# The slot list of an expert mixture built by TensorE products instead of 128 scattered stores, and the first expert operands loaded inside the front stage

## The reference

```python
dw = conv(q_lin, dw_w) + dw_b                     # 3 taps, by channel
off = tanh(pw_w @ gelu(dw) + pw_b) * 6
positions = clip(base + anchor + off, 0, q - 1)   # 16 heads x 12 samples
scores = qh . sample(kh, positions) / sqrt(16) - rel_scale * |rel|
out = softmax(scores) . sample(vh, positions)
...
idx = top_k(x @ Wr.T + br + biases_N, 2)          # 8 experts
h = x @ Wl1[e] + bl1[e];  a, b = halves of h      # 256 -> 2 x 512
y = (silu(a) * b) @ Wl2[e] + bl2[e]               # 512 -> 256
ffn = sum over the 2 chosen of weight * y
```

## Time and profile before

| what | value |
|---|---|
| median of 3 runs (lowest to highest) | 1495.42 us (1495.07 to 1499.51) |
| span of the profiled execution | 1494.3 us |
| what lies around its span | 1.1 us, taken as median less span; the profile gives no separate time of that execution |
| pass two of the front, steps 3 to 12 | from 165.4 to 309.9 us |
| end of the front block, first work of the mix block | 359.6 and 362.8 us |
| busy over the span | PE 91%, DVE 86%, ACT 55%, POOL 54% |
| DVE busy from 500 to 1200 us | 691.5 of 700 us |

### The profile page before, as it was taken

One profiled execution on the slowest core, in us unless ns is written; L12 is line 12 of the kernel. 1 busy time (PEld: TensorE's weight loads), 2 busy tenths in 40 slices (PEclk: granted clock), 3 DMA queues, 4 the chain that ended last, 5 costly groups with the idle time before them and its releaser, 6 DMA issues.

```text
span 1494.3 us, 35841 instructions
## 1 busy us (share of the span) xinstructions
PE 1361.6 (91%) x13687; PEld 1085.4 (73%) x13688; DVE 1280.2 (86%) x1504; ACT 823.8 (55%) x1889; POOL 804.3 (54%) x566
## 2 busy tenths in 40 slices
PE   5998899984799999999999998999999978797988
PEld 4864565653688888888888886887888856675766
DVE  7837655556699999999999999999999999999961
ACT  2547687864445555555555554554555436574655
POOL 1001477773587766767666877768686651311111
PEclk9999999985999999999999999999999988898999
DMA  7933366564957676768677666767777679999897
GB/s 231 352 130 101 115 203 208 166 222 158 287 122 224 170 232 161 222 161 235 183 204 214 168 179 160 214 159 201 196 190 221 133 178 232 250 218 246 217 246 148
DMA packets 203481, 293.52 MB, mean 196 GB/s; under 512 B 24833, under 2 KB 160261, under 8 KB 203123
## 3 DMA queue, kind: packets, MB, share of 16 engines
q0 software_dynamic: 65792, 146.59, 38.5%
q1 hardware_dynamic: 134915, 144.84, 33.6%
q10 hardware_dynamic: 2672, 0.83, 0.2%
HBM read 182.83 MB, written 117.74 MB: 201 GB/s over the span
## 4 chain that ended last, share of the span: by engine, by line
DVE 48%; DMA 8%; PE 8%; issue 6%; SPq 5%; POOL 0%; ACT 0%; POOLq 0%; DVEq 0%
DVE gslope L1647 11%; DVE parts L1643 11%; DVE parts L1603 8%; DMA band<-band_rows 7%; DVE expert_mem L1569 5%; PE pB L1480 3%; DVE parts L1615 3%; SPq L1121 2%; DVE parts L1619 2%; DVE parts L1622 1%; PE pA L1465 1%; PE pY L1490 1%; DVE gslope L1700 1%; SPq L1115 1%; DVE wgt L1708 1%
## 5 line engine op out<-in xcount | busy, mean ns | idle before, releaser
L1175 POOL DMA_INDIRECT moe_rows<-expert_mem,token_of x142 | 324.9, 2288 | 76.2 <-issue 47.9
L1446 PE MATMUL pA<-xsT,expert_mem 128*128 128x256 f32 x1136 | 264.5, 387 | 22.6 <-DMA expert_mem<-in_w_l 15.5
L1156 POOL DMA_INDIRECT expert_mem<-xn_rows,token_of x142 | 222.3, 1566 | 96.8 <-issue 74.2
L1452 PE MATMUL pY<-expert_mem 128*128 x1136 | 265.7, 387 | 0.0
L1446 PEld LDWEIGHTS pA<-xsT,expert_mem 128*128 128x128 f32 x1136 | 220.3, 195 | 55.9 <-issue 20.0
L1446 PE MATMUL pB<-xsT,expert_mem 128*128 128x256 f32 x1136 | 256.8, 379 | 0.0
L1452 PEld LDWEIGHTS pY<-expert_mem 128*128 128x128 f32 x1136 | 211.1, 191 | 42.3 <-issue 16.2
L1446 PEld LDWEIGHTS pB<-xsT,expert_mem 128*128 128x128 f32 x1136 | 215.8, 190 | 29.3
L1643 DVE SCALAR_TENSOR_TENSOR parts<-pos_pair,prob 128x768 f32<-128x768 f32 x256 | 228.0, 953 | 1.1
L1647 DVE TENSOR_REDUCE gslope<-parts 128x256 f32<-128x3072 f32 x64 | 214.7, 3354 | 2.2
L1297 ACT ACTIVATE expert_mem<-pA,b1sel 128x256 f32<-128x256 f32 x284 | 111.3, 474 | 135.3 <-issue 93.2
(11 more groups left out here) (197 smaller groups left out, 2036.3 us busy)
## 6 DMA issues: line engine op xcount, KB each, us to landing
expert_mem<-in_w_l POOLq DMA_DIRECT2D x71, 1024.0 KB, 7.0
band<-band_rows SPq DMA_DIRECT2D x256, 96.0 KB, 5.5
S_rows<-stage SPq DMA_DIRECT2D x64, 376.0 KB
band_rows<-wgt SPq DMA_DIRECT2D x12, 1536.0 KB, 7.1
pos_pair<-pos_rows SPq DMA_DIRECT2D x28, 384.0 KB, 7.7
xn_rows<-stage SPq DMA_DIRECT2D x16, 512.0 KB, 5.4
v_rows<-stage SPq DMA_DIRECT2D x16, 512.0 KB, 4.2
moe_rows<-zeros POOLq DMA_DIRECT2D x4, 2048.0 KB
```

The source lines that it names most:

```text
L1156: nc.gpsimd.indirect_dma_start(out=xs[:, u, s], out_offset=None, in_=dram["xn"], in_offset=bass.IndirectOffsetOnAxis(ap=keep["inv"][:, 2 * ...
L1175: nc.gpsimd.indirect_dma_start(out=dram["moe"], out_offset=bass.IndirectOffsetOnAxis(ap=keep["inv"][:, 2 * n + s:2 * n + s + 1], axis=0), ...
L1446: mm = nc.tensor.matmul(dst[:, c], w1[:, 1 - u, k, o * HID + c * P:o * HID + (c + 1) * P], xsT[:, k], start=(k == 0), stop=(k == KC - 1))
L1452: mm = nc.tensor.matmul(pY[:, s], hid[:, h, c, s * P:(s + 1) * P], w2[:, c, ds(e * D, D)], start=False, stop=(s == 1 and c == HC - 1))
```

## The change

One: the list is no longer written by GpSimd. In the steps 3 to 13 VectorE builds one-hot matrices of type bf16, four (choice, tile) columns at a time (a part; there are 32 parts, three in a step and two in step 13), and TensorE sums their products in the PSUM tile `pCount`: the row is the slot's low seven bits, the column its high part, one half holds the token's lane plus one and the other its tile number. In step 14 VectorE reads the sums (`tokens_of_slots`). Two: `expert_mem` is now allocated over both blocks, and shares memory with `kT` and `stage`. Inside the front GpSimd loads the first two pairs' first weights, as soon as step 7 has been scored, and gathers their rows; SyncE loads two of the four parts of `w2` in steps 8 and 9. Three: in the mix block SyncE issues the third part of `w2`, then `reload_slope(1)`, then the fourth; ScalarE starts with `evacuate_x(0)` and `take_expert(0, 0)` and does `prepare(0)` after them.

```diff
-            def scatter(some):
-                for c in some:
-                    nc.gpsimd.indirect_dma_start(
-                        out=dram["list"], out_offset=bass.IndirectOffsetOnAxis(ap=list_row[:, c:c + 1], axis=0),
-                        in_=token_i[:, c:c + 1], in_offset=None).then_inc(scattered, 16)
...
-            for q in range(4):
-                scatter(range(q * LISTED // 4, min((q + 1) * LISTED // 4, LISTED - 8)))
+            for q in range(2):
                 clear_moe(q)
-            scatter(range(LISTED - 8, LISTED))
+            pool.wait_ge(experts_known, 1)
+            pool.wait_ge(s_done, EARLY_FROM * GROUP)
+            for n in range(2):
+                e = pool.value_load(keep["tile_exp"][0:1, n:n + 1], min_val=0, max_val=EXPERTS - 1)
+                pool.dma_start(keep["w1"][:, 1 - n], io["w_l1"][ds(e, 1), :, :].rearrange("o (k p) n -> p (o k) n", p=P)).then_inc(
+                    keep["w1_loaded"][n], 16)
+            for q in range(2, 4):
+                clear_moe(q)
...
-            pool.wait_ge(scattered, 16 * LISTED)
-            pool.dma_start(spare_i[:], dram["list"].rearrange("(p n) o -> p (n o)", p=P)).then_inc(list_loaded, 16)
             pool.wait_ge(gates_stored, 16 * 4)
...
+            pool.wait_ge(tokens_known, 1)
+            for n in range(2):
+                for s in range(2):
+                    nc.gpsimd.indirect_dma_start(
+                        out=keep["xs"][:, n, s], out_offset=None, in_=dram["xn"],
...
+            def place_part(b):
+                if b < 0 or b >= LIST_PARTS:
+                    return
+                pe.wait_ge(hot_ready, b + 1)
+                for i in range(LIST_PART):
+                    mm = nc.tensor.matmul(pList, low_hot[b % 2][:, i], high_hot[b % 2][:, i].rearrange("p f n -> p (f n)"),
+                                          start=(b == 0 and i == 0), stop=(b == LIST_PARTS - 1 and i == LIST_PART - 1))
+                mm.then_inc(hot_used, 1)
...
+            def hot_part(b):
...
+                low, high, cols = low_hot[b % 2], high_hot[b % 2], slice(b * LIST_PART, (b + 1) * LIST_PART)
+                tile = b * LIST_PART % TILES
+                if b >= 2:
+                    dve.wait_ge(hot_used, b - 1)
+                V.tensor_tensor(low, place[:, None, 0:LOW].broadcast_to([P, LIST_PART, LOW]),
+                                slot_low[:, cols].unsqueeze(2).broadcast_to([P, LIST_PART, LOW]), ALU.is_equal)
+                chain(V.tensor_tensor(high[:, :, 1], place[:, None, :].broadcast_to([P, LIST_PART, HIGH]),
+                                      slot_high[:, cols].unsqueeze(2).broadcast_to([P, LIST_PART, HIGH]), ALU.is_equal))
+                chain(V.tensor_scalar(high[:, :, 0], high[:, :, 1], lane[:, 0:1], None, ALU.mult))
+                V.tensor_tensor(high[:, :, 1], high[:, :, 1], place[:, tile:tile + LIST_PART].unsqueeze(2).broadcast_to([P, LIST_PART, HIGH]),
+                                ALU.mult).then_inc(hot_ready, 1)
+
+            def tokens_of_slots():
+
+                dve.wait_ge(hot_used, LIST_PARTS)
...
+                hot_part((n - LIST_FROM) * PARTS_EACH)
                 if n + 2 < STEPS:
                     slopes_of_k(n + 2)
+                for i in range(1, PARTS_EACH):
+                    hot_part((n - LIST_FROM) * PARTS_EACH + i)
+                if n == STEPS - 2:
+                    tokens_of_slots()
...
-            sp.wait_ge(w1_loaded[0], 16)
-            for k in range(HC):
-                sp.dma_start(w2[:, k].rearrange("p (e n) -> p e n", e=EXPERTS),
-                             io["w_l2"].rearrange("e (k p) n -> k p e n", p=P)[k]).then_inc(w2_loaded, 16)
+            for k in range(EARLY_W2, HC):
+                keep["load_w2"](sp, k)
+                if k == EARLY_W2:
+                    reload_slope(1)
...
-            prepare(0)
             evacuate_x(0)
             take_expert(0, 0)
+            prepare(0)
```

More of the change, by code:

```diff
@@ L65 @@
 LISTED = TOPK * TILES
+LIST_PART = 4
+LIST_PARTS = LISTED // LIST_PART
+PARTS_EACH = 3
 COUNT_AT = 1
@@ L106 @@
 BAND_SKEW = BAND - 1
+W2_F, W1_F, HID_F = HC * EXPERTS * D, 2 * KC * 2 * HID, 4 * HC * PAIR
+ACT_F, XS_F, YS_F = 2 * HC * PAIR, 2 * 2 * XROW, 2 * 2 * D
+KT_PITCH = 8224
+W1_AT = KT_PITCH
+HID_AT = W1_AT + W1_F
+STAGE_AT = XS_AT = 2 * KT_PITCH
+ACT_AT = XS_AT + XS_F
+YS_AT = ACT_AT + ACT_F
+SHARED_F = YS_AT + YS_F
+EARLY_FROM = GROUPS_PER_SEQ
+EARLY_W2 = SEQ // (EXPERTS * D)
 PLACES = ("half products", "products", "half scores", "scores", "weights 0", "weights 1", "weights 2", "weights 3", "end")
@@ L181, in front_block @@
         wqk = sb("wqk", [P, KC, 2 * D])
-        wvr = sb("wvr", [P, KC, D + EXPERTS])
+        HOT_F = LIST_PART * HIGH
+        wvr_mem = sb("wvr", [P, max(KC * (D + EXPERTS), HOT_F)])
+        wvr = wvr_mem[:, 0:KC * (D + EXPERTS)].rearrange("p (k n) -> p k n", k=KC)
+        LOW_F = LIST_PART * LOW // 2
+        low_hot = [stage[:, u * LOW_F:(u + 1) * LOW_F].bitcast(BF16).rearrange("p (i n) -> p i n", n=LOW) for u in range(2)]
+        high_hot = [mem.bitcast(BF16).rearrange("p (i f n) -> p i f n", f=2, n=HIGH)
+                    for mem in (stage[:, 2 * LOW_F:2 * LOW_F + HOT_F], wvr_mem[:, 0:HOT_F])]
+        assert 2 * LOW_F + HOT_F <= 4 * GROUP_F - SX_F
         br_bc = sb("br_bc", [P, EXPERTS])
@@ L384, in _ @@
                     load_opening()
+                if n >= EARLY_FROM and n < EARLY_FROM + EARLY_W2:
+                    sp.wait_ge(s_done, EARLY_FROM * GROUP)
+                    keep["load_w2"](sp, n - EARLY_FROM)
             store_pos(STEPS - 2)
@@ L892, in _ @@
             V.tensor_copy(tile_row[:], keep["tile_exp"][:])
+            V.tensor_copy(place[:], place_i[:])
+            V.tensor_copy(lane[:], lane_i[:])
             chain(V.tensor_copy(base[:], base_i[:]))
@@ L1002, in mix_block @@
         pJ = [pY[:, 0], pO[:, 0]]
-        w1_loaded = [sem(f"w1_loaded{u}") for u in range(2)]
-        w2_loaded = sem("w2_loaded")
+        w1_loaded, w2_loaded, xs_loaded = keep["w1_loaded"], keep["w2_loaded"], keep["xs_loaded"]
         wo_loaded = sem("wo_loaded")
@@ L1009, in mix_block @@
         b_loaded = sem("b_loaded")
-        xs_loaded = [sem(f"xs_loaded{u}") for u in range(2)]
         xsT_done = sem("xsT_done")
@@ L1130, in _ @@
             sp.dma_start(bv[:], io["b_v"].rearrange("(k p) -> p k", p=P), allow_slow_non_contiguous=True).then_inc(wo_loaded, 16)
-            for it in range(1, 3):
-                reload_slope(it)
+            reload_slope(2)
             with sp.Fori(0, STEPS - BY_SP + 1) as it:
@@ L1190, in pair_io @@
                     take_y(n - LAG - 1, 1 - u)
-            for n in range(2):
-                load_xs(n, n)
-                load_w1(n, n)
             nc.gpsimd.memset(wgt[:], 0.0).then_inc(zeroed, 1)
@@ L1744, in build @@
         "moe": nc.dram_tensor("moe_rows", [TOKENS + SPARE, D], F32).ap(),
-        "list": nc.dram_tensor("slot_list", [SLOTS, 1], I32).ap(),
         "bias": nc.dram_tensor("bias_parts", [NB, EXPERTS, 2 * D], BF16).ap(),
@@ L1764, in build @@
         keep["posn"], keep["posw"] = keep["pos"][:, 0:PAIRS], keep["pos"][:, PAIRS:]
+        shared = keep["shared"] = sb("expert_mem", [P, SHARED_F])
+        keep["w2"] = shared[:, 0:W2_F].rearrange("p (k n) -> p k n", k=HC)
+        keep["w1"] = shared[:, W1_AT:W1_AT + W1_F].rearrange("p (u k n) -> p u k n", u=2, k=KC)
+        keep["xs"] = shared[:, XS_AT:XS_AT + XS_F].rearrange("p (u s c) -> p u s c", u=2, s=2)
+        assert TOKENS + 1 + 2 * REACH <= KT_PITCH and W1_F <= SEQ + 1 and XS_F <= 4 * GTOK * D // P - SX_SLOTS * (SUBS // 2) * S_ROW
+        for name in ("xs_loaded", "w1_loaded"):
+            keep[name] = [ctx.enter_context(nc.semaphore(f"{name}{u}")) for u in range(2)]
+        keep["w2_loaded"] = ctx.enter_context(nc.semaphore("w2_loaded"))
         for name in ("s_loaded", "posn_loaded", "pos_loaded"):
```

95 lines of the change are left out of this document (54 added, 41 removed).

## The result

| kernel | median us (lowest to highest, runs) | span of the profiled execution |
|---|---|---|
| before, beside it on the same chip | 1495.24 (1493.87 to 1499.51, 4) | 1494.3 |
| changed | 1535.53 (1534.23 to 1536.64, 4) | 1534.9 |

The ratio is 1.0259, 95% interval 1.0241 to 1.0277: the change costs 40.3 us. The forecast was 1527.5 us with a range from 1503 to 1547, so it was 8.0 us too low and within its range.

A forecast was written before the change was run, and what follows sets the result against it. TensorE was taken to fill pass two of the front, VectorE the mix block; with the change VectorE's ring sets the steps. 1494.3 + 41.1 (front) - 9.0 (mix block start) = 1526.4, plus 1.1 for the median: 1527.5 us, range 1503 to 1547.

The forecast's parts named there:

- VectorE's ring: Front, pass two: VectorE's chain from positions through slopes, parts, offset biases, TensorE's offsets and tanh sets steps of 18.2 us.
- Only the first gap can take added work: Front, step 6: only VectorE's 2.74 us idle before the first offset bias can absorb work; the other gaps stay.
- the second gap: Front, step 6: VectorE's 2.17 us idle before the second offset bias, a round trip said to stay however busy VectorE is.
- A part at 2.5 us: VectorE in the front: four one-hot instructions, priced from the nearest rows, take 2.5 us; three parts take 7.5 us.
- the cheap case: Rival, front: VectorE's instructions cost 0.41 us each, so TensorE's 16.6 us sets the step; 1511 us, chance 0.15.
- The offsets 1.57: Front, each step: TensorE's products between the two offset biases, counted in the 18.2 us sum at 1.57 us.
- the 18.2 of the sum: Front, ten steps 3 to 12: 18.2 us each, 182 against 144.5, so +37.5 us.
- The rival of half clock: Rival, front: TensorE's granted clock falls to 0.77 in every step, making its 16.6 us about 21; 1540 to 1560, chance 0.12.
- TensorE's path at 16.6 us: Front, each step: twelve new products add 2.1 us to 14.45, giving 16.6, shorter than VectorE's 18.2 us.
- Steps 13 and 14: End of the front: two parts lengthen step 13 by 2.0 us, six small list instructions lengthen step 14 by 1.6.
- The scattered stores at 0: Front: removing GpSimd's 128 stores, 132.8 us beside other work, gains 0 us, since the list's reader does not wait.
- The start of the mix block at -9.0: Mix block: four VectorE waits totalling 11.32 us go, the later prepare(0) costs 2.3 us; -9.0 us.

The follow-up runs named there:

- vec_filled: vec_dead with eight idle float32 products added on TensorE in the gap before the second offsets; 1529.18 us, ratio 1.022.
- vec_dead: loads_only with VectorE's 32 one-hot parts added as idle work that nobody reads, without TensorE's products; 1539.97 us, ratio 1.0273.
- pe_dead: loads_only with TensorE's 128 products added, reading two one-hot parts that VectorE builds once; 1511.95 us, ratio 1.0077.
- list_reordered: The changed kernel with each step's third part and step 14's list sums moved between the two offset biases; 1521.53 us, ratio 1.0176.
- loads_only: The changed kernel with the list written by GpSimd's scattered stores again, so only the change's second and third parts; 1491.74 us, ratio 0.9965.

## Why the prediction came out right, and where its sizes were off

1. *VectorE's ring sets the step: right.* Three dead parts alone give it (vec_filled 18.38, vec_dead 19.38), the products alone don't (pe_dead 15.63), and moving one part out of the ring takes the good steps to 16.4 (list_reordered). "Only the first gap can take added work" is right for the places where the change puts its parts, and wrong as it stands: in list_reordered the second gap took a whole part, and its wait fell from 1.72 to 0.15 us.
2. *A part at 2.5 us: right, 2.55, and 2.46 from start to start.* The choice of the float32 rows for bf16 products with a broadcast operand was the decisive one; it puts the cheap case (1511) out. The Trainium skill, Vector Engine (DVE) Microarchitecture Reference, section 5.1, says that a two-source instruction on 2-byte operands, one of them a single element read again and again, ran at the plain rate; the trace agrees (685 ns for 512 elements; 692 in float32). From positions to the first bias it was 14.2 us where the sum had 6.95 + 7.5 = 14.45.
3. *"The offsets 1.57" is the term that was mis-sized.* The forecast took TensorE's full-clock time from the earlier trace rows for a step in which I myself had TensorE idle about 1.6 us. Three steps with 1.54 us were 17.96 to 17.98 long, and the one with 2.73 was 19.2. The ten waits for them sum to 21.2 us, where ten of 1.72 would be 17.2: 4.0 us that the sum lacked. Over ten steps of 17.97 the ten measured ones are 5.9 us longer. The other 1.9 are nearly all VectorE work that the sum put at nothing: the row of `tile_exp` in step 3 delays positions by 1.25 us, and one more small instruction of `positions` adds 0.3 in each of two steps; before, VectorE's waits for TensorE took them in. The long row is this one:

```profile
167.73 1.85 DVE L929 SCALAR_TENSOR_TENSOR tile_exp<-tile_row,ends,tile_exp 1x71 f32<-1x71 f32 x6
```

Without these terms the step was 17.97 us and not the 18.2 of the sum, 2.3 us less over ten. That this made up for a part of what the sum lacked is luck.

The rival of half clock had the right mechanism and the wrong size: over a whole step the granted clock fell to between 0.91 and 0.96 and not to 0.77, in some steps and not in all, and what paid was only the one group of products behind the gap that stands on the ring. It was shown by filling the gap (vec_filled), and by the clock of 0.56 and 1.00 over the same eight products. TensorE's idle time was 2.1 to 2.6 us in the three steps shown, and not 1.6.

4. *TensorE's path at 16.6 us: not confirmed and not refuted.* The profiled pe_dead has 15.6, but it is the fastest of five executions, and by the estimate from the median above the path could be 16.7. This changed nothing, as the ring was above both. With the list reordered it would matter: the 16.4 us steps are close to it.
5. *Steps 13 and 14: +2.0 and +1.6 forecast, +2.7 and +1.1 measured. The scattered stores at 0: right.* vec_filled still has all 128 of them and steps of 18.38 us, the changed kernel has none and 18.56.
6. *The start of the mix block at -9.0: right to 0.1,* in the changed kernel and in loads_only, with the 2.3 us for the late `prepare(0)` confirmed by undoing it (93.5 against 95.7, so 2.2).
7. *Not in the sum: +4.3 us before the first part, +2.3 in the tail.* The first goes with a lower granted clock in the stretches from 100 to 140 and from 140 to 160 us. Those stretches of the kernel before, and then of the changed one:

```profile
100.00:140.00 40.00, 34.28 (x580) 18.48 (x578) 22.23 (x33) 28.68 (x48) 0.00 (x0) 0.96 0.19 69
140.00:160.00 20.00, 17.73 (x359) 11.02 (x360) 14.30 (x36) 12.25 (x25) 4.61 (x4) 0.91 0.57 132
```

```profile
100.00:140.00 40.00, 35.39 (x523) 17.95 (x521) 20.99 (x29) 25.95 (x45) 0.00 (x0) 0.91 0.18 65
140.00:160.00 20.00, 16.62 (x293) 10.43 (x292) 13.81 (x30) 12.67 (x24) 4.70 (x4) 0.83 0.51 112
```

pe_dead has 0.96 and 0.91 like before, and its `tanh` of step 2 is at 163.5; list_reordered has 0.96 and 0.83, and 164.9; vec_dead and vec_filled have 0.91 and 0.83, and 166.3 and 167.0. Up to step 3 list_reordered has the program of the changed kernel, and still lies 2.7 us earlier, so at least that much changes from one execution to another. What makes the clock fall there in some executions stays open; so does the tail.

The prices side by side, span by span: forecast 41.1 - 9.0 = 32.1, measured 40.6. Of the 8.5 between them 4.3 are the first steps, 2.2 the ten steps, 0.2 steps 13 and 14, -0.5 step 15 and the barrier, 2.3 the tail. Nothing in the sum stood for the first steps or the tail; the width of the range covered these 6.6 us, no argument did. The ten steps are off by 2.2 and not by the 3.6 of (18.56 - 18.2) x 10, since the kernel before has 145.9 by the `tanh` rows and 144.5 by the stretches of rows 1.

## What to carry to other kernels

Before moving work onto an engine with idle time, see which of its idle stretches lie in a round trip through other engines: these stay, whatever comes in front of them, and only work placed inside them is free. Here 128 stores that nobody waited for were replaced by 7.5 us a step on the ring, of which the first gap took less than half; moving one part into the round trip gave back 12 to 14 us of the 40. The early loads were worth about 5 us alone (interval 1 to 10), and should be kept without the list. And when a change makes an engine idle in front of a product that others wait for, take that product at its slower time at the upper end of the sum.

## What the runs showed of the hardware that I had not expected

- More work can take less time. The kernel with VectorE's parts and no products took 1539.97 us and steps of 19.38; with useless products in TensorE's gap it took 1529.18 and steps of 18.38. After an idle stretch of 3.26 us the eight offset products took 2.90 us, at a granted clock of 0.50; after 1.53 us they took 1.54 in one step (1.00) and 2.73 in another (0.56).
- TensorE can stand in the middle of a row of small products with nothing named as the cause, for 2.27 and 3.16 us here, and the products behind it then run slow (clock 0.82 over the step of the second). In one group of runs every kernel took 10% longer, and the profile of one shows stalls of up to 27.4 us in the front, with the DMA engines a quarter busy.
- Twelve bf16 products of 284 columns cost a full TensorE 0.95 us a step together in the profiled execution, the fastest of five, where their time lines show three times 0.65.
